# Softmax scaling on POOL, FFN's hidden units in one piece, row maximum ahead of the query statistics

## What is computed

```python
slots = q_mu + jnp.exp(q_logsig) * noise            # noise = layernorm(x)
for _ in range(3):
    prev = slots
    q = _ln(slots, lnq_g, lnq_b) @ wq + bq
    logits = jnp.einsum('bnd,bkd->bnk', k, q) / scale
    attn = jax.nn.softmax(logits, axis=-1) + EPS_ATTN      # over the slots
    attn = attn / jnp.sum(attn, axis=1, keepdims=True)     # over the context rows
    upd = jnp.einsum('bnk,bnd->bkd', attn, v)
    slots = upd @ wu + bu + prev
    h = _ln(slots, lnm_g, lnm_b) @ w1 + b1
    slots = gelu(h) @ w2 + b2 + slots
    slots = _ln(slots + cond[:, None, :], lnp_g, lnp_b)
x = x + slots
h = gelu(layernorm(x) @ ternary(W_fc).T)                   # 256 -> 1024
x = x + layernorm(h, ln_w, ln_b) @ ternary(W_proj).T       # 1024 -> 256
```

## Time and profile before

| | us |
|---|---|
| median of three runs | 339.01 (336.94 to 339.3) |
| the profiled execution | 339.19, of which the traced span 337.3 |
| busy PE, DVE, ACT, POOL | 316.9, 292.9, 235.6, 202.2 |
| rounds (first middle product of round 0 to last low product) | 49.1 to 253.2 |
| FFN (first fc to last result) | 249.2 to 334.4 |

### The profile page before, as it was taken

The page is one execution under the profiler, slowest core; times in us unless marked ns, Lnnn a source line. Parts: engine busy times, 40 slices in busy tenths (PEclk is TensorE's granted clock), DMA queues, the critical chain, the costliest instruction groups (busy, mean ns, idle before and its releaser), DMA issues. The chain is left out here.

```text
span 337.3 us, 6560 instructions
## 1 busy us (share of the span) xinstructions
PE 316.9 (94%) x1758; PEld 261.0 (77%) x1758; DVE 292.9 (87%) x851; ACT 235.6 (70%) x563; POOL 202.2 (60%) x385
## 2 busy tenths in 40 slices
PE   8899999999999989999998999799976899999994
PEld 8787888888887878888887788687853577767773
DVE  3699977899899889998999899999998789999874
ACT  2368986967467867785589674855638588898881
POOL 3168966255689764568987547377754944444341
PEclk9999999999999999999999999999999599999999
DMA  7988000000000000000000000000000000000001
GB/s 274 329 320 357 1 1 2 0 0 2 2 0 2 0 2 2 0 3 1 0 2 0 1 2 1 0 3 1 0 2 0 1 34 31 33 31 0 32 34 62
DMA packets 5311, 13.22 MB, mean 39 GB/s; under 512 B 672, under 2 KB 672, under 8 KB 4896
## 3 DMA queue, kind: packets, MB, share of 16 engines
q1 hardware_dynamic: 4160, 10.88, 8.6%
q10 hardware_dynamic: 1120, 1.98, 1.6%
HBM read 10.76 MB, written 2.10 MB: 38 GB/s over the span
## 5 line engine op out<-in xcount | busy, mean ns | idle before, releaser
L290 DVE BATCH_NORM_STATS2 stats<-S 128x6 f32<-128x256 f32 (+1 forms) x112 | 42.0, 416 | 9.3 <-DMA S<-ctx 3.5
L341 PE MATMUL ps_mid<-XT,KT 128*128 128x256 f32 x192 | 46.1, 383 | 3.4 <-ACT XT L357 3.4
L341 PE MATMUL ps_low<-V,PR 128*128 128x257 f32 x192 | 46.2, 383 | 1.7 <-DVE PR L863 1.7
L341 PE MATMUL ps_low<-wn,GT 128*128 128x256 f32 x192 | 45.7, 381 | 0.8 <-ACT GT L639 0.8
L341 PE MATMUL ps_mid<-XT,wt 128*128 128x256 f32 x192 | 45.5, 380 | 0.7 <-ACT XT L357 0.7
L341 PEld LDWEIGHTS ps_low<-V,PR 128*128 128x128 f32 x192 | 36.0, 190 | 8.4 <-DVE PR L863 3.5
L636 ACT ACTIVATE PR<-ps_mid,nmax 128x256 f32<-128x256 f32 x48 | 22.3, 471 | 27.3 <-DVE nmax L873 27.2
L341 PEld LDWEIGHTS ps_low<-wn,GT 128*128 128x128 f32 x192 | 36.1, 190 | 6.7 <-ACT GT L639 1.9
L341 PEld LDWEIGHTS ps_mid<-XT,KT 128*128 128x128 f32 x192 | 34.6, 190 | 8.4 <-ACT XT L357 4.6
L308 POOL TENSOR_TENSOR lnm_ab<-lnm_mv,mhalf 128x2 f32<-128x2 f32 x24 | 17.2, 715 | 38.9 <-DVE lnm_mv L298 38.9
L357 ACT ACTIVATE XT<-ps_t 128x512 f32<-128x512 f32 x56 | 33.1, 591 | 9.2 <-PE ps_t L333 9.2
(11 more groups left out here) (124 smaller groups left out, 706.4 us busy)
## 6 DMA issues: line engine op xcount, KB each, us to landing
S<-ctx SPq DMA_DIRECT2D x8, 256.0 KB, 3.8
X<-x SPq DMA_DIRECT2D x8, 256.0 KB, 3.4
out<-X SPq DMA_DIRECT2D x8, 256.0 KB, 2.0
rowv<-rows SPq DMA_DIRECT2D x1, 1920.0 KB, 9.9
wf<-w_fc_t SPq DMA_DIRECT2D x1, 1024.0 KB, 11.8
wf<-w_proj_t SPq DMA_DIRECT2D x1, 1024.0 KB, 13.8
wt<-w_tr ACTq DMA_DIRECT2D x1, 512.0 KB, 4.2
wn<-w_nat ACTq DMA_DIRECT2D x1, 512.0 KB, 5.8
```

The costliest lines, as they stand in the source:

```text
L290: dve.bn_stats(ln.st[:, at, j, 0:6], tiles[:, j]).then_inc(ln.stats_done, 1)
L341: last = pe.matmul(dst(m), lhs_t[:, c, m * P:(m + 1) * P], rhs[:, c, 0:n], start=(c == 0), stop=(c == 1))
```

## The change

1. The scaling of `PR` goes from VectorE to POOL, at the same step, in front of everything else that POOL does in it.
2. FFN's hidden units are handled as one piece of 1024: `fc` writes both banks of `ps_low[rt]`, with one Gelu, one GC, one square and no halves of their sums; `hidden_t` writes `ps_mid[h]` and waits for the low half of the previous block. The first FFN block starts one step later (`FFN_STEP`).
3. VectorE takes the row maximum ahead of the query statistics.

The diff, without the allocation of `gsum` and `qsum`, which become one column a block:

```diff
@@ -281,7 +281,7 @@
 T_FFN = B + ROUNDS * STEPS


-FFN_STEP = STEPS
+FFN_STEP = STEPS + 1
...
@@ -419,10 +419,10 @@
     def rstd_g(r, rt):
         if not early(r):
             pool.wait_ge(o_done, r - 1)
-        pool.wait_ge(sq_done, 2 * r + 2)
+        pool.wait_ge(sq_done, r + 1)
         pool.sem_inc(pool_held, 1)
-        pool.tensor_scalar(grstd[:, rt, 0:1], qsum[:, rt, 0:1], qsum[:, rt, 1:2], H * LN_EPS,
-                           ALU.add, ALU.add).then_inc(g_chain, 1)
+        pool.tensor_scalar(grstd[:, rt, 0:1], qsum[:, rt:rt + 1], 1.0, H * LN_EPS,
+                           ALU.mult, ALU.add).then_inc(g_chain, 1)
...
@@ -460,6 +460,14 @@
             pool.wait_ge(c_ready, B)
         if t == 0 and not last and s < 2:
             ln_coef(pool, lni, B - 2 + s, s)
+        if it := item(t, s, 2, last):
+            r, half, b = it
+            if half == 0:
+                pool.wait_ge(rinv_ready, r * B + (b + 1))
+                pool.sem_inc(pool_held, 1)
+                for j in range(J2):
+                    pool.tensor_scalar(PR[:, b % 4, j], PR[:, b % 4, j], rinv[:, b, j:j + 1], EPS_ATTN,
+                                       ALU.mult, ALU.add).then_inc(attn_ready, 1)
         if last:
...
@@ -551,37 +559,35 @@
             act.wait_ge(f1_ready, 4 * b - 4)
         act.activation(XTh[:, u].rearrange("p c k -> p (c k)"), ps_t[0][:], ACT.Copy).then_inc(xth_ready, 1)

-    def gelu_half(r, rt, h):
-        act.wait_ge(f1_ready, 2 * r + (h + 1))
+    def gelu(r, rt):
+        act.wait_ge(f1_ready, 2 * r + 2)
         if not early(r):
-            act.wait_ge(gc_done, 2 * r - 2)
-        act.activation(Gf[:, rt, h * HALF:(h + 1) * HALF], ps_mid[h][:], ACT.Gelu,
-                       accum_out=gsum[:, rt, h:h + 1]).then_inc(gelu_done, 1)
-
-    def square_half(r, rt, h):
+            act.wait_ge(gc_done, r - 1)
+        act.activation(Gf[:, rt], ps_low[rt][:].rearrange("p h n -> p (h n)"), ACT.Gelu,
+                       accum_out=gsum[:, rt:rt + 1]).then_inc(gelu_done, 1)
+
+    def square(r, rt):
         act.wait_ge(gneg_ready, r + 1)
         if not early(r):
             act.wait_ge(grstd_ready, r - 1)

-        act.activation(flat(XH, 2 * rt + h), Gf[:, rt, h * HALF:(h + 1) * HALF], ACT.Square, bias=gneg[:, rt:rt + 1],
-                       accum_out=qsum[:, rt, h:h + 1]).then_inc(sq_done, 1)
+        act.activation(XH[:, 2 * rt:2 * rt + 2].rearrange("p b j d -> p (b j d)"), Gf[:, rt], ACT.Square,
+                       bias=gneg[:, rt:rt + 1], accum_out=qsum[:, rt:rt + 1]).then_inc(sq_done, 1)

     def high_half(r, rt, h):
         act.wait_ge(tg_ready, 2 * r + (h + 1))
         if not early(r):
             act.wait_ge(o_ready, r - 1)
-        act.activation(GTh[:, rt, 4 * h:4 * h + 4].rearrange("p t k -> p (t k)"), ps_low[rt][:, h],
+        act.activation(GTh[:, rt, 4 * h:4 * h + 4].rearrange("p t k -> p (t k)"), ps_mid[h][:],
                        ACT.Copy).then_inc(gth_ready, 1)

     def ffn(b, u, rt, last=None):
         r = 2 * b + rt
-        gelu_half(r, rt, 0)
-        gelu_half(r, rt, 1)
+        gelu(r, rt)
         if not (isinstance(r, int) and r == 0):
             high_half(r - 1, 1 - rt, 0)
             high_half(r - 1, 1 - rt, 1)
-        square_half(r, rt, 0)
-        square_half(r, rt, 1)
+        square(r, rt)
         if rt == 0 and (last is None or last < B - 1):
             copy_high(b + 1, 1 - u)

...
@@ -770,25 +776,23 @@
                           XTh[:, u].rearrange("p c k -> p (c k)"), ALU.subtract).then_inc(xtl_ready, 1)

     def centre(r, rt):
-        dve.wait_ge(gelu_done, 2 * r + 2)
+        dve.wait_ge(gelu_done, r + 1)
         if not early(r):
-            dve.wait_ge(sq_done, 2 * r - 2)
-        dve.tensor_scalar(gneg[:, rt:rt + 1], gsum[:, rt, 0:1], gsum[:, rt, 1:2], -1.0 / H,
-                          ALU.add, ALU.mult).then_inc(gneg_ready, 1)
+            dve.wait_ge(sq_done, r - 1)
+        dve.tensor_scalar(gneg[:, rt:rt + 1], gsum[:, rt:rt + 1], -1.0 / H, None, ALU.mult)\
+           .then_inc(gneg_ready, 1)
         if not early(r):
             dve.wait_ge(tg_ready, 2 * r - 2)
         dve.wait_ge(gneg_ready, r + 1)
-        for h in range(2):
-            dve.scalar_tensor_tensor(out=GC[:, rt, h * HALF:(h + 1) * HALF],
-                                     in0=Gf[:, rt, h * HALF:(h + 1) * HALF], scalar=gneg[:, rt:rt + 1],
-                                     in1=rowv[:, ROW_LNW + h * HALF:ROW_LNW + (h + 1) * HALF],
-                                     op0=ALU.add, op1=ALU.mult).then_inc(gc_done, 1)
+        dve.scalar_tensor_tensor(out=GC[:, rt], in0=Gf[:, rt], scalar=gneg[:, rt:rt + 1],
+                                 in1=rowv[:, ROW_LNW:ROW_LNW + H],
+                                 op0=ALU.add, op1=ALU.mult).then_inc(gc_done, 1)

     def low_half(r, rt, h):
         dve.wait_ge(gth_ready, 2 * r + (h + 1))
         if not early(r):
             dve.wait_ge(o_ready, r - 1)
-        dve.tensor_tensor(GTl[:, rt, 4 * h:4 * h + 4].rearrange("p t k -> p (t k)"), ps_low[rt][:, h],
+        dve.tensor_tensor(GTl[:, rt, 4 * h:4 * h + 4].rearrange("p t k -> p (t k)"), ps_mid[h][:],
                           GTh[:, rt, 4 * h:4 * h + 4].rearrange("p t k -> p (t k)"), ALU.subtract)\
            .then_inc(gtl_ready, 1)

@@ -855,23 +859,16 @@
             if half == 0:
                 dve.wait_ge(mid_read, ring(r, half, b) * 2 + (2 + 2 * RING))
                 dve.reciprocal(rinv[:, b], rsum[:, b]).then_inc(rinv_ready, 1)
-        if it := item(t, s, 2, last):
-            r, half, b = it
-            if half == 0:
-                dve.wait_ge(rinv_ready, r * B + (b + 1))
-                for j in range(J2):
-                    dve.tensor_scalar(PR[:, b % 4, j], PR[:, b % 4, j], rinv[:, b, j:j + 1], EPS_ATTN,
-                                      ALU.mult, ALU.add).then_inc(attn_ready, 1)
-        if at_q:
-            r, half, b = at_q
-            dve.wait_ge(y_ready, r * (J2 * B) + (J2 * b + J2))
-            bn_rows(dve, lnq, b, Y[:, b])
         if it := item(t, s, 1, last):
             r, half, b = it
             if half == 0:
                 dve.wait_ge(mid_ready, ring(r, half, b) + (1 + RING))
                 dve.tensor_reduce(nmax[:, b], ps_mid[b % 2][:].rearrange("p (j k) -> p j k", j=J2), AX.X,
                                   ALU.max, negate=True).then_inc(max_ready, 1)
+        if at_q:
+            r, half, b = at_q
+            dve.wait_ge(y_ready, r * (J2 * B) + (J2 * b + J2))
+            bn_rows(dve, lnq, b, Y[:, b])
         if at_q and not fill:
             sum_q()
         part = None
...
@@ -1019,28 +1016,27 @@
     def fc(b, u, r, rt):
         if rt == 0:
             pe.wait_ge(xtl_ready, b + 1)
+        if early(r):
+            pe.wait_ge(low_read, 2 * (T_FFN - 1 + r) + 2 * RING)
+            pe.wait_ge(lnb_copied, 3)
+        else:
+            pe.wait_ge(gelu_done, r - 1)
+        for h in range(2):
+            parts = [(c, part) for c in range(C2) for part in (XTh, XTl)]
+            for k, (c, part) in enumerate(parts):
+                last = pe.matmul(ps_low[rt][:, h], part[:, u, c, rt * P:(rt + 1) * P],
+                                 WfT[:, c, h * HALF:(h + 1) * HALF], start=(k == 0), stop=(k == 3))
+            last.then_inc(f1_ready, 1)
+
+    def hidden_t(r, rt):
+        pe.wait_ge(gc_done, r + 1)
         for h in range(2):
             if isinstance(r, int) and r == 0:
                 pe.wait_ge(mid_read, 2 * T_FFN + 2 * RING)
             else:
-                pe.wait_ge(gelu_done, 2 * r + (h - 1))
-            parts = [(c, part) for c in range(C2) for part in (XTh, XTl)]
-            for k, (c, part) in enumerate(parts):
-                last = pe.matmul(ps_mid[h][:], part[:, u, c, rt * P:(rt + 1) * P],
-                                 WfT[:, c, h * HALF:(h + 1) * HALF], start=(k == 0), stop=(k == 3))
-            last.then_inc(f1_ready, 1)
-
-    def hidden_t(r, rt):
-        for h in range(2):
-            pe.wait_ge(gc_done, 2 * r + (h + 1))
-            if not early(r):
-                pe.wait_ge(gtl_ready, 2 * r + (h - 3))
-            elif h == 0:
-                pe.wait_ge(low_read, 2 * (T_FFN - 1 + r) + 2 * RING)
-            elif r == 0:
-                pe.wait_ge(lnb_copied, 3)
+                pe.wait_ge(gtl_ready, 2 * r + (h - 1))
             for k in range(4):
-                last = pe.transpose(ps_low[rt][:, h, k * P:(k + 1) * P],
+                last = pe.transpose(ps_mid[h][:, k * P:(k + 1) * P],
                                     GC[:, rt, (4 * h + k) * P:(4 * h + k + 1) * P], ident[:])
             last.then_inc(tg_ready, 1)

```

More of the change, by code:

```diff
@@ L134, in halves @@
             return vf[:, at:at + n // 2].bitcast(F16)
-        gsum = sb("gsum", [2, 2])
-        qsum = sb("qsum", [2, 2])
+        gsum = sb("gsum", [2])
+        qsum = sb("qsum", [2])
         gneg = sb("gneg", [2])
```

## The result

The changed kernel takes 340.99 us (median of 9 runs, 340.57 to 343.06); the kernel before took 338.89 beside it (9 runs, 336.94 to 339.3). The ratio is 1.0092, with a 95% interval from 1.0069 to 1.0116: slower by 0.9%, which is less than the 1% that the chances took as their bound, yet clear of the measurement's scatter. The prediction was 339.9 within 336.0 to 344.0.

The account below looks back on a forecast made before the run. The prediction took TensorE, busy 94% of the span, as the bound. Its terms, 1.5 + 1.9 - 1.2 - 1.7 - 0.45 + 0.7 - 0.6 + 0.6 = +0.75, on 339.19 gave 339.9 us, range 336.0 to 344.0.

Parts of the forecast that it names:

- Price of the scaling: One scaling of 256 elements on POOL takes 0.40 us, a pair 0.8 us, with ends 0.4 and 1.45.
- rival 1: POOL scales at its add rate, 1.45 us a pair, giving 343.0 us; chance 0.20.
- items 4 and 5 cost nothing: Steady half of a round: POOL's scaling is ready 0.3 us before the low product needs it, so no loss.
- T+5.75: Steady half: scaling ready 5.75 us after the start T of a step's transposes, against the low product at T+6.07.
- Item 6: Steps 7 and 8, rounds 0 and 1: TensorE waits 0.85 us for the scaling; +1.9 us in two rounds.
- Step 18: First two rounds: the earlier maximum removes the late copy before the middle product, 0.58 us twice, -1.2 us.
- First scaling: Round 0: the scaling waits behind POOL's eight condition additions, low product near 57.2, +1.5 us (+1.1 to +2.1).
- Last round, lnb, tail: Late starts at steps 8 to 10 shrink, -1.7; lnb row's copy stops holding TensorE, -0.45; last hidden transposes delay proj(14), +0.6.
- Seam: Entry into FFN: VectorE's chain delays the next sample's rows, +0.7 us (-1 to +2); the 2.7 us low-clock loss stays.
- rival 4: Seam into FFN denser, clock stays at 2.4 GHz, 2.7 us back, if h(0) starts before 256: 335.2 us; chance 0.14.
- Rivals 2 and 3: 2: POOL not late in ternary steps, 338.0, chance 0.13; 3: hidden transposes stall each FFN block, +4, 344, chance 0.13.
- FFN loop: One-piece Gelu and GC win 0.5, lose 0.42 us: 0.1 a pair of blocks, -0.6 us in all (0 to -1.9).

Follow-up runs that it names:

- Part 3 alone: The kernel before with only the row maximum moved ahead of the query statistics: 338.21 us, ratio 0.9977.
- part 2 alone: The kernel before with only FFN's hidden units in one piece, its other buffers and its later first block: 336.33 us, ratio 0.9935.
- parts 2 and 3: The changed kernel with the scaling of PR back on VectorE: 335.72 us, ratio 0.9919 against the kernel before.
- fastest version: The kernel with both orders, but all eight condition additions on POOL stand behind the scalings of steps 2 to 5: 332.24 us, ratio 0.9816.
- both orders: The changed kernel with POOL's condition additions spread behind the first scaling and each S shift one step later, behind the next scaling: 333.96 us, ratio 0.9869.
- spread additions: The changed kernel with POOL's eight condition additions spread over later steps, not one block ahead of the first scaling: 339.11 us with only this edit, ratio 1.0017.
- parts 1 and 2: The changed kernel with the query statistics ahead of the row maximum again: 340.48 us, ratio 1.0095 against the kernel before.
- S shift late: The changed kernel with only POOL's S shift one step later, right behind the scaling: 335.09 us, ratio 0.9931 against the kernel before.

## Why the prediction came out as it did

The time was right within 1.1 us (as a change it is +2.1 where I had +0.75), but as a sum of errors of both signs, which is luck. Without the fall of the clock the last proj came 2.5 us late instead of 0.75. The 1.75 between are +3.4 for the waits on POOL, -3.0 at the seam, +0.6 in the loop, +0.25 at step 18, and 0.5 of small terms, 0.35 of it the prologue's.

**Price of the scaling: near, its weight wrong.** I took 0.40 us for one, it is 0.48 (pair 0.94, not 0.8). The bounds held, and rival 1's rate of 1.45 a pair did not come. The failed sentence is "items 4 and 5 cost nothing": the margin there was 0.3 us, and three small things used it up. Against the forecast T+5.75 the scaling of item 4 in round 1 was done at T+6.33 (142.82): VectorE's aggregates came 0.29 later than the T+2.3 that I gave them, the pair took 0.14 more, coefficients and S shift 0.15 more. The product started 0.31 late and, begun after a stop, took 0.1 longer: 0.42. A margin of 0.3 built from four terms that are each known to 0.1 is no cover.

**Item 6: right mechanism, size off.** The aggregates were forecast 3.15 us behind the low product's end and came 3.23 behind. Behind them stood 3.4 us of POOL work; it took 4.03 (148.10 to 152.13), with L309 at 0.33 and the scaling pair at 1.08 beside VectorE's work. 0.85 became 1.49, twice. (The term says +1.9 for the two rounds, but 0.85 twice is 1.7.) The signs named for the profile had waits at items 6 and 7 and none at 4 and 5; in rounds 0 and 1 they came at 4 and 6.

**Item 2 overlooked.** I had only the steady half in view. In rounds 1 and 2 items 0 to 4 run beside the last steps of the round before, where POOL also makes Y and the query coefficients: 0.5 us, twice. In round 1 of the changed kernel POOL works without a break from the Y of 129.82 to the end of item 2's scaling, and TensorE waits for it:

```profile
129.82 1.41 POOL L487 TENSOR_TENSOR Y<-XH,rowv 128x256 f32<-128x256 f32 x2
...
133.65 0.94 POOL L469 TENSOR_SCALAR PR<-PR,rinv 128x256 f32<-128x256 f32 x2
```

```profile
134.65 2.00 PE L341 MATMUL ps_low<-V,PR 128*128 128x257 f32 x8 [0.29 <-POOL PR L469]
```

Together the waits for the scaling on POOL at items 4 and 6 of rounds 0 and 1 cost 3.85 us where I had 1.9, and those at item 2 of round 1 and at items 2 and 4 of the last round 1.5 us where I had nothing.

**Step 18.** 1.2 forecast, 0.95 measured, but credited to part 3. Part 3 alone gained the forecast 0.6 between T(20) and T(21), yet lost 0.28 just before: with the maximum first, statistics and aggregation take longer, and the scaling behind them came late (0.17 us of wait for it at 121.01 in its trace). The prediction priced each part against the kernel before; it never asked what part 3 is worth once the scaling has left VectorE. It would have been seen: the prediction itself names the scaling first among what stands in front of the late maximum.

**First scaling.** 1.5 forecast, 1.66 measured without the fall of the clock. That TensorE's idle time could also cost it its clock at this place was not among the terms, though I had priced just that at the seam.

**Last round, lnb, tail.** -1.7, -0.45 and +0.6 forecast; -1.84, -0.35 and +0.39 measured. (The three late starts of the last round add up to 2.6, not to the 2.8 of the prediction.) The tail is as described: the transposes of block 15 wait for the low halves of block 14 and proj(14) for them.

```profile
332.59 1.28 DVE L795 TENSOR_TENSOR V<-ps_mid,V 128x512 f16<-128x512 f32 x2
```

```profile
333.41 1.16 PE L1039 MATMUL ps_mid<-ident,KT 128*128 128x128 f32 x8 [1.27 <-DVE V L795]
334.41 3.66 PE L1049 MATMUL ps_t<-w,V 128*128 128x256 f16 x32
```

**Seam: wrong sign, +0.7 for -2.3.** The rows of the changed kernel, TensorE, then a window:

```profile
259.06 1.90 PE L1027 MATMUL ps_low<-w,V 128*128 128x512 f16 x8 [0.49 <-DVE S L896]
263.73 1.97 PE L1039 MATMUL ps_mid<-ident,KT 128*128 128x128 f32 x8 [2.77 <-DVE KT L787]
265.49 2.47 PE L1027 MATMUL ps_low<-w,V 128*128 128x512 f16 x8
268.23 1.16 PE L1039 MATMUL ps_mid<-ident,KT 128*128 128x128 f32 x8 [0.27 <-DVE V L795]
269.38 0.66 PE L333 MATMUL ps_t<-ident,PR 128*128 128x128 f32 x4
269.87 1.91 PE L1049 MATMUL ps_t<-w,V 128*128 128x256 f16 x16
```

```profile
262.00:268.00 6.00, 4.23 (x16) 2.55 (x16) 4.29 (x8) 5.61 (x12) 3.54 (x4) 0.72 0.00 0
268.00:274.00 6.00, 5.77 (x43) 4.38 (x44) 5.74 (x14) 4.27 (x9) 5.36 (x11) 1.00 0.00 0
```

Up to the rows of the next sample I was near: with the 6.12 us that it enters late, 262.90 became 269.38, +0.36 where I had +0.7. What I left in, the 2.7 us of the low clock, is what went. The clock did fall, and h(0) (1.97 us, against 1.04 later on) and fc(2) (2.47 against 1.89) ran in it; but the next transposes, at 268.23, had to wait 0.27 us for VectorE even so. From 268 on, with proj(0) and fc(3), the clock is at 2.4 GHz, and proj(0) takes 1.91 us instead of 3.62. From the rows of the next sample to fc(4) it is 6.58 us instead of 9.24. I had written that the same idleness brings the same loss. The loss depends on which work falls into the low stretch, and that moved. The other traces bear it out: the seam gave 2.61 us in part 2 alone, where the clock fell, and 2.61 in parts 2 and 3, where it stayed up; 2.30 in the changed kernel with the fall, and 2.29 without it in the fastest version. This was rival 4's price (2.7 back) without rival 4's condition: h(0) started at 257.6 once the lateness of 6.12 is taken off, as the forecast chain had it (257.5), not before 256. Rivals 2 and 3 failed: POOL was late in the ternary steps, and hidden_t did not stall each block.

**FFN loop: -0.6 for -0.03.** A pair went from 9.55 to 9.28 us in the steady part, more than the 0.1 I had. (The 1.05 ns an element used for GC stands in none of the prediction's rows; 751 to 1286 ns for 512 more elements is 1.04.) But one block lost 0.9 first. VectorE and POOL in parts 2 and 3, and the TensorE wait that follows:

```profile
267.57 2.18 DVE L779 SCALAR_TENSOR_TENSOR KT<-KT,gneg,rowv 128x1024 f32<-128x1024 f32 x1
```

```profile
267.40 1.27 POOL L442 TENSOR_TENSOR X<-X,lnb_out 128x512 f32<-128x512 f32 x1
```

```profile
270.80 1.25 PE L1038 MATMUL ps_mid<-ident,KT 128*128 128x128 f32 x8 [0.33 <-DVE V L787]
```

and the same block in the kernel with both orders:

```profile
266.36 1.28 DVE L791 SCALAR_TENSOR_TENSOR KT<-KT,gneg,rowv 128x1024 f32<-128x1024 f32 x1
```

```profile
266.44 2.33 POOL L442 TENSOR_TENSOR X<-X,lnb_out 128x512 f32<-128x512 f32 x1 [0.20 <-issue]
```

In the first POOL's addition began 0.17 us ahead and VectorE's GC took 2.18; in the second GC began 0.08 ahead and took 1.28, and the addition, which has time, took 2.33. At this block it is the same in every kernel with GC in one piece: in all six where the addition began first, GC took 2.18 to 2.20 us and the loop gained 0.03 to 0.21 us; in all three where GC began first (those with the spread additions) it took 1.28 and the loop gained 0.93 to 0.95.

## What to carry to other kernels

When work moves to another engine, its duration matters less than what stands ahead of it in that engine's program: the same scaling on POOL cost 3.4 us behind additions that nobody needed yet, and with these put behind it, together with parts 2 and 3, the kernel became 6.5 us faster than before. Price each part of a joint change against the kernel with the other parts in, since two remedies for one hole pay once. And a margin of a few tenths put together from several durations is not a cover; give it a price.

## What the hardware showed

- VectorE and POOL, each with an operation that reads two SBUF tensors, took turns rather than shared: whoever began first kept its time (1.28 and 1.27 us), the other took 0.9 to 1.06 longer. A start 0.08 us ahead was enough. Nine traces show it, six one way and three the other. The GPSIMD Engine Reference of the Trainium skill (Specifications) names contention with VectorE instructions that have two SBUF inputs; the trace agrees, with the 0.9 to 1.06 us above.
- POOL's one-input operation on 128x256 fp32 took 0.482 us, against 0.345 to 0.353 undisturbed on VectorE and 0.727 for POOL's two-input add. The factor is 1.4.
- TensorE's clock fell to 1.2 GHz behind a wait of 1.91 us in one execution and stayed at 2.4 GHz behind the same wait of 1.90 us in another; TensorE came 1.68 us later in the first. In the kernels where that wait was removed (12, 6 and 5 runs) the runs lie within 1.2, 0.6 and 0.8 us. In two that keep it, single executions lie apart, with a lower mean granted clock: 341.88 and 342.09 us at 0.990 against 339.85 to 340.59 at 0.995 (parts 1 and 2), and 337.0 at 0.988 against 334.86 to 335.28 at 0.993 to 1.0 (S shift late). Where their clock fell was not traced.
- What a stretch at the low clock costs depends on the work in it: some 2 us at the seam of the kernel before, nothing that can be seen at the seam of the changed one.
- Twice the elements in one instruction saved about 0.2 us on either engine: Gelu 1.026 us against 2 x 0.597, GC 1.286 against 2 x 0.751.
